# Smaller weight DMAs and a gate loop with one projection of lag, in an attention and feed-forward layer on eight cores

## What is computed

```python
q, k, v = x @ Wq, x @ Wk, x @ Wv            # 16 heads of 64, 64, 128
s = clip(x @ Ws, -32, 32)                   # 16 heads of 64 slots
o = _chunk_abc(q, k, v, s)                  # two scans over the tokens
g = x @ Wg
o = o * rsqrt(mean(o**2, -1) + EPS) * g_norm_weight
o = o * (g * sigmoid(g))                    # the gate
x = layernorm(x + o @ Wo)
h = relu(x @ W1 + b1)
alpha = softmax(h @ W2 + b2)                # 8 weights for each token
out = einsum('bsk,bskd->bsd', alpha, U (V x))
x = layernorm(x + out)
```

## Time and profile before

| | us |
|---|---|
| median of the two runs shown | 1919.35 |
| the two runs | 1900.76 and 1937.93 |
| the profiled execution | 1900.64 |
| its span on the slowest core (core 4) | 1899.1 |
| spans of the eight cores | 1879.0 to 1899.1 |

### The profile page before, as it was taken

One profiled execution on the slowest core, in us unless ns is written; L12 is line 12 of the kernel. 1 busy time (PEld: TensorE's weight loads), 2 busy tenths in 40 slices (PEclk: granted clock), 3 DMA queues, 4 the chain that ended last, 5 costly groups with the idle time before them and its releaser, 6 DMA issues.

```text
span 1899.1 us, 18758 instructions; the slowest of 8 cores (1879.0 to 1899.1 us)
## 1 busy us (share of the span) xinstructions
PE 1305.6 (69%) x6800; PEld 642.8 (34%) x6800; DVE 532.7 (28%) x886; ACT 409.0 (22%) x552; POOL 230.4 (12%) x220
## 2 busy tenths in 40 slices
PE   2459898978995555687585758968555476768562
PEld 1124444434443333333242323424333333324230
DVE  2012333242002222344431272000222234352145
ACT  0000000001114444421210132101444432020013
POOL 2100000000002111242100001100111134110000
PEclk9669999989995555788887768979555588879775
DMA  9950100013406000477965149970500055893502
GB/s 180 180 89 22 45 23 23 23 37 77 65 1 89 1 1 1 58 113 145 218 111 89 26 74 233 171 117 12 78 1 1 1 89 89 178 183 61 89 1 89
DMA packets 61515, 146.25 MB, mean 77 GB/s; under 512 B 7536, under 2 KB 12016, under 8 KB 56048
## 3 DMA queue, kind: packets, MB, share of 16 engines
q0 software_dynamic: 54800, 102.90, 35.3%
q1 hardware_dynamic: 5472, 33.76, 5.3%
q10 hardware_dynamic: 1152, 8.39, 1.1%
HBM read 237.45 MB, written 8.39 MB: 129 GB/s over the span
## 4 chain that ended last, share of the span: by engine, by line
PE 48%; DMA 18%; DVE 14%; ACT 8%; issue 6%; POOL 4%; DVEq 1%; ACTq 0%; POOLq 0%
PE fb L245 46%; DMA wvb<-wv 6%; DMA wob<-wo 4%; DMA wkb<-wk 3%; DMA w1b<-w 3%; PE tb L245 2%; POOL wbf L265 2%; DMA wsb<-ws 1%; ACT rbuf L265 1%; DVE x1bufs L265 1%; DVE st L265 1%; DVE sm L265 1%; ACT wrw L265 1%; ACT cfm L265 1%; POOL obs L265 1%
## 5 line engine op out<-in xcount | busy, mean ns | idle before, releaser
L245 PE MATMUL fb<-w1b,x2fm 128*128 128x512 bf16 x512 | 129.8, 415 | 35.9 <-DMA w1b<-w 35.9
L245 PE MATMUL fb<-wvb,xpf 128*128 128x512 bf16 x512 | 119.6, 394 | 30.8 <-DMA wvb<-wv 30.8
L245 PE MATMUL fb<-wob,ofm 128*128 128x512 bf16 x512 | 118.0, 394 | 19.0 <-DMA wob<-wo 19.0
L245 PE MATMUL fb<-wvb,xmf 128*128 128x512 bf16 x512 | 118.6, 395 | 14.6 <-DMA wvb<-wv 14.6
L245 PE MATMUL fb<-wgb,xmf 128*128 128x512 bf16 x512 | 118.8, 395 | 8.2 <-DVE gsc L265 5.4
L265 DVE TENSOR_TENSOR okb<-fb,rbuf 128x256 f32<-128x256 f32 x32 | 13.6, 425 | 309.9 <-ACT rbuf L265 168.8
L245 PE MATMUL fb<-wsb,xpf 128*128 128x512 bf16 x256 | 71.8, 444 | 32.8 <-DMA wsb<-ws 20.6
L245 PEld LDWEIGHTS fb<-w1b,x2fm 128*128 128x128 bf16 x512 | 52.0, 104 | 106.6 <-issue 58.0
L245 PEld LDWEIGHTS fb<-wvb,xpf 128*128 128x128 bf16 x512 | 50.7, 100 | 96.9 <-issue 42.5
L265 DVE TENSOR_TENSOR s1f<-s1f,fb 64x256 f32<-64x256 f32 (+1 forms) x48 | 24.1, 502 | 209.0 <-PE fb L245 207.3
L245 PEld LDWEIGHTS fb<-wob,ofm 128*128 128x128 bf16 x512 | 51.4, 101 | 84.8 <-issue 29.4
(11 more groups left out here) (149 smaller groups left out, 1882.7 us busy)
## 6 DMA issues: line engine op xcount, KB each, us to landing
strip<-x_main SPq DMA_DIRECT2D x24, 1024.0 KB, 9.8
wvb<-wv POOLq DMA_DIRECT2D x16, 1024.0 KB, 35.2
wgb<-wg POOLq DMA_DIRECT2D x16, 1024.0 KB, 20.2
wob<-wo POOLq DMA_DIRECT2D x16, 1024.0 KB, 22.6
w1b<-w POOLq DMA_DIRECT2D x16, 1024.0 KB, 23.4
strip<-x_pre SPq DMA_DIRECT2D x8, 1024.0 KB, 6.7
wqb<-wq POOLq DMA_DIRECT2D x8, 1024.0 KB, 31.1
y<-x1bufs ACTq DMA_DIRECT2D x8, 1024.0 KB, 5.6
```

The source lines that it names most:

```text
L245: t.matmul(o, l, r, start=a, stop=b, is_transpose=(True if tpp else None)))
```

## The change

Three edits. Weight loads are issued in DMAs of two row blocks by default, where it was four, in both helpers. A load spreads over up to eight semaphores, where it was four; this holds for the three loads at the start too, which were in DMAs of two row blocks before. In the gate stage a gate runs one projection behind, where it was two, and `gsc` has two buffers instead of three.

```diff
-        def load_w(name, dram, rows, cols, col0=0, ncols=None, per_dma=4,
+        def load_w(name, dram, rows, cols, col0=0, ncols=None, per_dma=2,
                    side="left"):
...
-            sems = [next_wsem() for _ in range(min(npc, 4))]
+            sems = [next_wsem() for _ in range(min(npc, 8))]
...
         def load_w_into(buf, dram, rows, cols, col0=0, ncols=None,
-                        per_dma=4, waits=()):
+                        per_dma=2, waits=()):
...
-            sems = [next_wsem() for _ in range(min(npc, 4))]
+            sems = [next_wsem() for _ in range(min(npc, 8))]
...
-            gsc2 = [AR.alloc("gsc", [128, GV], F32) for _ in range(3)]
-            gsc2_free = [None, None, None]
+            gsc2 = [AR.alloc("gsc", [128, GV], F32) for _ in range(2)]
+            gsc2_free = [None, None]
...
                         gv = vop(lambda v, g=g, cn=cn, bk=bk, c=c: v.tensor_copy(
-                            gsc2[c % 3].ap(0, 128, g * 512, cn),
+                            gsc2[c % 2].ap(0, 128, g * 512, cn),
                             bk[g][0:128, 0:cn]),
-                            waits=[mG_of[c], gsc2_free[c % 3]]
-                            + gsc2[c % 3].birth)
+                            waits=[mG_of[c], gsc2_free[c % 2]]
+                            + gsc2[c % 2].birth)
...
                 def g_gate(c, vh):
-                    gsc = gsc2[c % 3]
+                    gsc = gsc2[c % 2]
...
-                    gsc2_free[c % 3] = sg
+                    gsc2_free[c % 2] = sg
...
-                for c in range(NHC + 2):
+                for c in range(NHC + 1):
                     if c < NHC:
                         g_proj(c)
-                    if c - 2 >= 0:
-                        otb_free = g_gate(c - 2, vh)
+                    if c - 1 >= 0:
+                        otb_free = g_gate(c - 1, vh)
                     if c < NHC:
                         g_evac(c)
```

More of the change, by code:

```diff
@@ L1175, in build_program @@
                 AR.freebuf(ovhh[vh], toks=bPAT)
-            for b in (msq, otb, obs, sgs, gsc2[0], gsc2[1], gsc2[2]):
+            for b in (msq, otb, obs, sgs, gsc2[0], gsc2[1]):
                 AR.freebuf(b, toks=bPAT)
```

## The result

| | before | after |
|---|---|---|
| median of the runs, us | 1902.11 (6 runs, 1899.9 to 1940.35) | 1925.07 (7 runs, 1922.35 to 1927.71) |
| the profiled execution | 1900.64 | 1927.39 |
| its span on the slowest core | 1899.1 (core 4) | 1925.6 (core 4) |
| spans of the eight cores | 1879.0 to 1899.1 | 1912.5 to 1925.6 |

The changed kernel is slower, by a factor of 1.0127 (95% interval 1.0113 to 1.0141), some 24 us. I had put it 8 us above the profiled execution of before.

The account below looks back on a forecast made before the run. PE was taken to bound the kernel, working through stages or waiting for weight row blocks. From 1900.6, arrival -6.0, POOL issue +5.3 and gate stage +8.6 gave 1908.5 us; range 1893 to 1930.

Parts of the forecast that it names:

- Issue time on POOL: First wg load as the attention loop begins: eight issues delay the mask multiply 2.67 us in each half, +5.3 us.
- The gate stage: Four gate passes: one gate less in the tail, but a hole in front and slow clock behind it, +8.6 us.
- rival (a): Gate stage: PE's clock holds through the holes, so the stage is even and the total 1899.9 us; chance 0.20.
- (e): Gate stage: the new lag does not change PE's order of work in time, total 1899.9 us; chance 0.02.
- The semaphores: Weight loads on POOL: chunks wait for the load before, but DMA engines don't run dry; costed at nothing.
- The arrival of weights: Exposed wo, w1, wv, wk loads: last byte lands as before, four matmuls remain instead of eight, -6.0 us.
- What PE has left to do: Behind an exposed load's last chunk: four matmuls of the first token block, not eight; 0.7 to 1.3 us saved each.
- Rival (b): Five exposed loads: finer chunks keep PE's clock up, saving 1.86 us each, total 1899.2 us; chance 0.08.
- (c): Small w2 load: last chunk waits for the b1 load and comes late, PE waits 10 us per half, 1928; chance 0.08.
- (d): Eight exposed loads, 32 more DMAs: each holds the engines a fixed time, 2001 us at 2.9 each; chance 0.04.
- The runs of before: Whole kernel: median 1919.35 between two differing runs, so a median of few could come some 19 us above the sum.
- The range: Whole kernel: 1893 to 1930 us, from terms' bounds 1896 to 1912, widened for two rivals and the runs' distance.

Follow-up runs that it names:

- e5_rows2: Kernel before with DMAs of two row blocks only for weights loaded in whole rows, up to eight semaphores for a load; 1917.58 us (1898.41 for before beside it).
- g2_contig4: Kernel before (four row blocks) with wv, wg, wo and w1 stored as two contiguous halves; no ratio, four runs too far apart, lowest 1903.92 us.
- e9_halves1: Kernel before with single-row-block DMAs for column halves, sixteen semaphores, whole rows still in four blocks; 1933.5 us.
- f1_halfstrip: Kernel before, loading only the half of each residual strip that the column half needs (512 KB, not 1024) in the wo stage; ratio 0.9946.
- e1_lag1: Kernel before with only the gate loop's lag of one and two gsc buffers; run twice, ratios 1.0101 and 1.0069.

## Why the prediction was partly wrong

- **Issue time on POOL: right.** +5.3 by sum, 5.3 measured in the changed kernel. POOL's timeline of after, to be held against the earlier trace rows:

```profile
1338.10 5.70 POOL L233 DMA_DIRECT2D wgb<-wg  x8 [78.36 <-ACT qtm L265]
1343.82 1.16 POOL L265 TENSOR_TENSOR abf<-arw,lmb 128x512 bf16<-128x512 bf16 x1
```

- **The gate stage: right.** +8.6 by sum; 9.2 in the changed kernel, 9.7 alone. Holes of 6.63 and 3.35 us where I had 7.0 and 4.2, one wait of 5.31 in the tail where I had about 5, a clock of 0.50 behind a hole as I had said, and the matmuls there slower still (9.29 and 9.53, I had 8.76). So rival (a), that the clock holds, is false, and (e) too.
- **The semaphores: right at nothing**: with sixteen of them the landings and the time stay. In pass 1 POOL's issues from 830.84 (5.75 us) end before its next multiply at 843.16.
- **The arrival of weights: wrong**, and this is nearly the whole miss. I had -6.0; it is +12.0, 18.0 of the 18.6 us by which the spans' 26.5 pass my 7.9. The step that failed is the sentence "Their rate does not depend on the chunk". I compared 512 KB of wk (3.14 us) with 1024 KB of w1 (6.22) and found the same rate. These two differ in a second thing: wk is read in whole rows, w1 in half rows with gaps. For wk's kind the sentence holds (e5_rows2), and for halves of four blocks the gaps cost nothing (g2_contig4). It is two blocks together with gaps that costs, a pairing that before never has: its loads of two blocks, ahead of the first loop, are of whole rows. w1's chunks of 512 KB came 3.50 us apart, not 3.11.
- **What PE has left to do: right and of no use.** Four matmuls stood behind the last chunk, but the chunk landed 1.3 and 2.1 us (w1) and 4.3 and 5.5 us (wo) later. For w1 in half 0 the two came out even (the stretch behind it: -0.2). And a load that was not waited for, the first wv half of half 1, is now waited for, because it queues in a chain where the loss adds up.
- **Rival (b)** (finer chunks keep the clock up): false, each four matmuls behind a wait took up to 1.87 us. **(c)** (w2 late): false. POOL's and PE's timelines of after show its last issue at 975.38, and PE's use with no wait for a DMA:

```profile
975.38 0.72 POOL L233 DMA_DIRECT2D w2b<-w  x1 [1.79 <-DMA w2b<-w]
...
995.72 0.34 PE L245 MATMUL fb<-w2b,hfm 128*128 128x8 bf16 x8 [1.62 <-DVE hfm L265]
```

- **(d)** (a fixed time for each DMA) had right that loads land later, for a wrong reason. The landings of the chain (+6.6), wo (+4.3, +5.5) and w1 (+2.1, +1.3) are 19.8 us for 32 more DMAs, 0.6 each and short of the 0.95 at which it decides; and whole rows show 0, single blocks no more than double ones. The rule of at least 1 MiB for each DMA in the Trainium skill (page "DMA: Bandwidth & Descriptors", section "Rules for kernel authors") would have warned me, if it means the bytes written (512 KB; 1 MiB is read). But loads of whole rows, of the same size, lost nothing here.
- **The runs of before**: the median of six, 1902.11, is near the sum's base of 1900.6; the 19 us that I allowed for between them were not needed.
- **The range: held by luck.** The measured 1925.07 lies within 1893 to 1930, but the terms' bounds ended at 1912. The rest was there for (c) and for the distance of the runs of before, and neither is what happened. (Those bounds add up to 1895 and 1911, and the lower bound of the arrival term to -5.0; I had 1896, 1912 and -4.9. Nothing hangs on it.)

## What to carry over

A rate read from one load holds for loads of the same shape in memory: before cutting a DMA in two, look whether its rows lie together, and if not, compare a load of the same pitch or measure one. A full DMA share says that the engines are taken, not that they move data at their rate; read the GB/s beside it. And what cutting can win, the work left behind the last chunk (0.9 us here), is small beside the 1 to 7 us by which it moved the last chunk itself. How late a load lands also depends on the neighbour core, so compare landings at the same distance of the two.

## What the runs showed of the hardware that I had not expected

A load in DMAs of two row blocks lost time when each 4 KB read was followed by 4 KB passed over (w1 31.3 us against 28.8, both at less than 3 us from the neighbour core), none at four blocks, and no more at one (29.9 to 30.9 on the six cores of e9_halves1 that were within 5 us of their neighbour in half 1).

Two neighbour cores that load at the same time slow each other (w1 in four blocks: 28.8 us, and 25.0 when they are over 10 us apart): in e9_halves1 cores 0 and 1 issued the second w1 half of half 1 14 us apart and had it after 26.3 and 26.1 us.

PE's granted clock was 0.81 in dense stretches of some executions, neither the low level nor the high one: 16 matmuls took 4.38 us instead of 3.62, in a stage that was 10.7 us longer. It came by pairs of cores: in f1_halfstrip the same stage took 81.7 to 81.8 us on cores 2, 3, 6 and 7 (mean clock 0.70) and 71.1 to 71.9 on cores 0, 1, 4 and 5 (0.82 and 0.83). PE's timelines of e1_lag1 and of before:

```profile
984.64 4.38 PE L245 MATMUL fb<-v2tb,x2fm 128*128 128x512 bf16 x16
```

```profile
995.11 3.62 PE L245 MATMUL fb<-v2tb,x2fm 128*128 128x512 bf16 x16
```

The Trainium skill (page "TensorE: Matmul & The Clock Gate", Part 1) states a limit of 13/16 of the clock once three cores of a die run dense matmuls. The 0.81 agrees with it. But before runs the same stage dense on all eight cores at 1.00, and in f1_halfstrip two cores of a die had it and two had not, so the page's condition alone does not say when it comes; what does stays open.
